# Gated cross-attention: the scalar engine's exponential moved ahead of the three copies of the unit before it

## What is computed

```
q = qn @ Wq * scale                          # 16 heads of 64
k, v = split(media @ Wkv)                    # 1500 keys
sim = einsum('bhid,bhjd->bhij', q, k)
sim = where(media_mask, sim, neg_inf)
attn = softmax(sim, axis=-1)
out = einsum('bhij,bhjd->bhid', attn, v)
x = x + tanh(attn_gate) * (out @ Wo)
x = x + tanh(ff_gate) * (gelu(layernorm(x) @ W1) @ W2)
```

## Time and profile before

| | |
|---|---|
| median of 3 runs | 2667.14 us (2666.37 to 2675.62) |
| the profiled execution's own time | 2673.55 us |
| its span, first to last instruction | 2671.8 us |
| PE busy | 2521.3 us (94% of the span) |
| DVE, ACT, POOL busy | 1572.3, 1258.2, 590.3 us |
| mean granted TensorE clock | 0.95 of full speed |
| the two stretches of gated attention | about 217 to 860 us and 1930 to 2570 us |

### The profile page before, as it was taken

The page is one execution under the profiler, slowest core; times in us unless marked ns, Lnnn a source line. Parts: engine busy times, 40 slices in busy tenths (PEclk is TensorE's granted clock), DMA queues, the critical chain, the costliest instruction groups (busy, mean ns, idle before and its releaser), DMA issues.

```text
span 2671.8 us, 43128 instructions
## 1 busy us (share of the span) xinstructions
PE 2521.3 (94%) x16890; PEld 2048.4 (77%) x16890; DVE 1572.3 (59%) x4305; ACT 1258.2 (47%) x2148; POOL 590.3 (22%) x729
## 2 busy tenths in 40 slices
PE   7779999999999988988999999899999999999998
PEld 4647999999999667965666666545599999999975
DVE  3146777777776233446766766521577777777741
ACT  2125555555555211116777777520455555555521
POOL 0013444444440004200000000000244444444200
PEclk8789999999999997569999999899999999999999
DMA  8511111111100200001000010101111111111010
GB/s 273 153 49 53 53 39 41 53 38 41 53 27 1 80 18 1 1 3 45 24 24 24 24 34 4 34 31 58 38 41 53 39 41 53 39 41 53 1 48 14
DMA packets 36103, 116.34 MB, mean 44 GB/s; under 512 B 4598, under 2 KB 18526, under 8 KB 35534
## 3 DMA queue, kind: packets, MB, share of 16 engines
q1 hardware_dynamic: 33438, 101.30, 12.2%
q10 hardware_dynamic: 2464, 12.29, 1.8%
HBM read 112.66 MB, written 0.92 MB: 43 GB/s over the span
## 4 chain that ended last, share of the span: by engine, by line
PE 86%; DVE 8%; ACT 2%; DMA 2%; issue 1%; POOL 0%; SPq 0%; ACTq 0%; DVEq 0%; POOLq 0%
PE bank L864 19%; PE bank L851 17%; PE bank L876 11%; DVE n_scores L1635 4%; PE bank L1516 4%; PE bank L1503 3%; PE bank L1528 3%; PE bank L1744 3%; PE bank L1088 2%; PE bank L1073 2%; PE bank L1272 2%; PE bank L683 2%; PE bank L1081 2%; PE bank L1754 2%; PE bank L1253 2%; PE bank L504 2%
## 5 line engine op out<-in xcount | busy, mean ns | idle before, releaser
L924 ACT CAST p_T_high<-bank 125x512 fp32r<-125x512 f32 x672 | 350.6, 595 | 546.8 <-PE bank L876 546.8
L1004 DVE TENSOR_TENSOR p_T_low<-bank,p_T_high 125x512 fp32r<-125x512 f32 x576 | 362.2, 684 | 183.0 <-ACT p_T_high L924 179.5
L864 PE MATMUL bank<-p_T_high,keys_nat_high 125*128 125x256 f32 x1536 | 419.3, 283 | 1.7 <-ACT inverse L931 1.7
L962 DVE CUSTOM_DVE_ANT_0 scores<-bank,mask 128x500 f32<-128x500 f32 x672 | 418.2, 672 | 1.5 <-PE bank L851 1.5
L864 PE MATMUL bank<-p_T_high,keys_nat_low 125*128 125x256 f32 x1536 | 419.1, 283 | 0.0
L934 ACT ACTIVATE scores<-scores,row_max 128x1500 f32<-128x1500 f32 x224 | 353.6, 1578 | 6.5 <-DVE row_max L967 6.5
L876 PE MATMUL bank<-ident,scores 128*125 128x128 f32 x2688 | 330.7, 272 | 1.3 <-ACT scores L934 1.3
L864 PE MATMUL bank<-p_T_low,keys_nat_high 125*128 125x256 f32 x1152 | 325.4, 282 | 0.0
L876 PEld LDWEIGHTS bank<-ident,scores 128*125 128x125 f32 x2688 | 314.2, 188 | 2.7 <-ACT scores L934 2.5
L1635 DVE CUSTOM_DVE_ANT_0 n_scores<-bank,n_zeros 112x500 f32<-112x500 f32 x384 | 237.5, 675 | 127.3 <-PE bank L1503 127.3
L864 PEld LDWEIGHTS bank<-p_T_high,keys_nat_high 125*128 125x128 f32 x1536 | 291.4, 190 | 10.1 <-ACT inverse L931 2.2
(11 more groups left out here) (209 smaller groups left out, 3649.2 us busy)
## 6 DMA issues: line engine op xcount, KB each, us to landing
ctx_T<-in_ctxT SPq DMA_DIRECT2D x40, 750.0 KB, 4.2
ctx_nat<-in_ctx SPq DMA_DIRECT2D x32, 672.0 KB
q_and_o<-in_ctxT SPq DMA_DIRECT2D x16, 750.0 KB, 10.4
q_and_o<-in_ctx ACTq DMA_DIRECT2D x16, 672.0 KB
mask_bytes<-in_mask SPq DMA_DIRECT2D x32, 187.5 KB, 3.0
n_ctx_T<-in_ctxT SPq DMA_DIRECT2D x8, 750.0 KB, 4.4
weights<-in_L_W SPq DMA_DIRECT2D x4, 1024.0 KB, 9.7
ctx_nat<-in_ctx SPq DMA_DIRECT2D x32, 78.0 KB
```

The source lines that it names most:

```text
L864: m = e.matmul(psum[6 + g % 2][:, 0:256], KNs[i][b % 2][0:KP, cols], PTs[j][g % 2][0:KP, k, :], start=(k == 0 and n == 0), stop=(k == KT - ...
L924: e.copy(PTs[0][g % 2][0:KP, 4 * c:4 * c + 4, lo:lo + 128], psum[3 + c][0:KP, :].rearrange("p (k r) -> p k r", k=4)).then_inc(s_eh, 1)
L962: e.tensor_tensor_reduce(out=SB[u % 2][:, c * CHK:(c + 1) * CHK], in0=psum[c][:, 0:CHK], in1=mb[:, c * CHK:(c + 1) * CHK], scale=1.0, scal ...
L1004: e.tensor_tensor(low, psum[3 + c][0:KP, :].rearrange("p (k r) -> p k r", k=4), high.bitcast(F32), ALU.subtract).then_inc(s_el, 1)
```

## The change

In every slot of `act_cross` the exponential of unit s is issued first, and after it the copies (and the inverse copy) of unit s-1. Nothing is added or taken away, and the programs of the other engines are as they were.

```diff
             for s in range(U + 1):
                 u = s - 1
+                if s < U:
+                    on.wait_ge(*x.negmax(s))
+                    e.activation(SB[s % 2], SB[s % 2], ACT.Exp, bias=mx[:, s % 4, 3:4],
+                                 accum_out=mx[:, s % 4, 4:5]).then_inc(s_ex, 1)
                 if u >= 0:
                     g = group_of(u)
                     lo = 128 * ((u % RT) % 2)
...
                         if g >= 2:
                             on.wait_ge(*x.o_out(g - 2))
                         e.copy(inverse[g % 2][:, 0:n], psum[6 + g % 2][:, 0:n]).then_inc(s_in, 1)
-                if s < U:
-                    on.wait_ge(*x.negmax(s))
-                    e.activation(SB[s % 2], SB[s % 2], ACT.Exp, bias=mx[:, s % 4, 3:4],
-                                 accum_out=mx[:, s % 4, 4:5]).then_inc(s_ex, 1)
```

## The result

The changed kernel takes 2749.96 us (median of 4 runs, 2746.35 to 2753.74), the kernel before 2666.76 us (4 runs): a ratio of 1.0312, 95% interval 1.0291 to 1.0333. That is 83 us more.

What follows compares the result with a forecast made beforehand. PE was taken to bound the kernel at 5.71 us a slot; a ring of 6.06 us adds 41.4 us a layer, 83 for two: 2673.55 + 83 = 2756.5 us profiled, 2750 as a median; range 2720 to 2800.

Steps and rivals of the forecast that it cites:

- What bounds the kernel: Layer 1's attention: PE busy 610.00 of 610.00 us, 5.71 us a slot, and waiting for no exponential.
- the ring: Gated attention: closed loop of maxima, negated maximum, exponential, copies, low parts, next maxima; 6.06 us a slot against PE's 5.71.
- from exponential to copy: Step on ACT between the starts of the exponential and of the copy behind it, taken as 1.54 us.
- Start to start or full lengths: Pricing of one turn: distances between starts give 6.06 us and 2750; full instruction lengths give 6.29 us and 2800.
- The inverse copy and DVE's results at no cost: ACT's inverse copy (0.41 us) and DVE's result of a group (0.42 us) were to add nothing to a slot.
- PE's waits: PE waits up to 1.1 us for the inverse, three times a batch: 2.4 us idle a batch, PE busy 94%.
- its rival: PE joins the ring: restarts costing 1.1 us would overrun by 0.9 us a batch, 29 us, 2779 us; chance 0.12.
- The clock: Rival: PE's idling lowers its clock for a tenth of the time, 98 us in all, 2848 us; chance 0.05.
- The sum: Gated stage of one layer: last unit's maxima move from 852.8 to 894.2 us, 41.4 us, 83 for two layers.

## Why the prediction was right

- **What bounds the kernel, and that an earlier exponential frees nobody:** right. PE was busy for all of 610 us, and the kernels in which the exponential is early but the ring short come to 1.0015 and 1.0030.
- **The ring and its length:** forecast 6.06 us, found 6.04, link by link 1.91, 0.19, 1.54, 0.60 and 1.80 against 1.91, 0.19, 1.54, 0.62 and 1.80. Only the step from copy to low part was 0.02 us too long. The one link with no row in the gated stage, from exponential to copy, had been taken from layer 2 and holds to the hundredth. That this ring is the cause is shown, not argued: opened in every second slot it costs nothing, a known length put in comes out whole (71 us for 72), and a shorter link ahead of the copies takes nearly all the loss away.
- **Start to start or full lengths:** the full lengths would have given 6.29 a slot and 2800 us; the 6.048 us between the negated maxima decides for the distances between starts. The rule of the Trainium skill that I had named ("Perfetto Trace Analysis", "Optimizing Scalar/DVE Operations") says the same, and the runs bear it out. The choice was worth 50 us.
- **The inverse copy and DVE's results at no cost:** right, with less to spare than forecast, which priced a group's result alone (0.42 us). For a single unit three instructions stand there, and the last of them lasted 1.22 or 1.24 us in place of 0.29 in 14 of the 15 batches from 240 to 880 us (609.81 in the timeline), each time beside a POOL instruction (here `keys_nat_low`, 609.59 to 610.88). It ended 0.32 us before the low parts started. The prediction had no term for this; that it stayed hidden is luck.
- **PE's waits:** 46 in 640 us, that is, in 15.1 batches of 42.3 us: three in a batch, right in place and number. The forecast was 2.4 us of idle in a batch and PE busy for 94%; PE's rows show 23.7 us of idle, 1.6 in a batch, and 96%. A batch is 42.3 - 40.0 = 2.3 us longer all the same. The 0.8 us that idle doesn't show are three restarts of 0.27 us, in which the profile has PE busy. The prediction gave them no price, named 1.1 us in its rival and saw the ring in danger above 0.6. At 0.27 the ring keeps its pace. That price was learnt from the kernel with one copy ahead; the runs with the longer ring show that the waits are no part of the cost.
- **The clock:** granted in full in both stages (PEclk 1.00), with PE busy for 96% of them. That rival did not come about.
- **The sum:** forecast 41.4 us for a layer, found 38.2 and 39.2. The turn is 0.012 us shorter than taken, 1.3 us over 109 turns. Of the other 1.9 us of layer 1, 1.7 lie in its first slots: the negated maxima of units 0 and 1 are at 219.97 and 221.95 now, 1.98 us apart, where they were 3.70 apart before, when the score matmuls of unit 1 started 0.42 us apart, at the lower clock, and not 0.23; the ring starts with unit 1. The prediction had taken that slower start over from the trace of before. In layer 3 that start was at full speed before as well (1923.15 and 1925.13, 1.98 apart). That the medians are 83 apart, just as forecast, while the stages grew by 77 in the profiled executions, is some luck.
- **Three steps of the experiments' expectations failed by size:** PE's restart after a wait (61 us where 31 were forecast), DVE's instruction meeting POOL's (144 us for 74), and the link behind half an exponential (0.92 us for 0.74). None touches the verdict on the change.

## What to carry to other kernels

Before swapping two instructions on an engine that has slack, follow each engine's own order through the semaphores and ask whether the swap closes a ring: here ACT was busy for 57% of the stage and DVE for 74% before the change, and yet the two together set the pace once each had to wait for the other in every slot. Add up the ring from start to start, and compare it with the slot of the engine that bounds; a fraction over costs that fraction in every slot, a fraction under costs nothing. Then look for further loops: the order with one copy ahead had a ring under PE's slot and still cost 61 us, through the inverse. In a stage that another engine bounds, an instruction that is early for its reader is worth nothing, while the one that it pushes back may be the next that somebody waits for.

## What the runs showed of the hardware that was not expected

- A DVE addition with both operands in SBUF (128 x 256) took 414 ns on average in one order and 727 ns in another. Where POOL was at work when it began, it ended 0.27 to 0.29 us after POOL's instruction (42 of 99) and lasted up to 1.61 us. With one operand in PSUM it lasted 0.41 or 0.42 us in all of 97, met by POOL or not, and the low parts (an operand in PSUM) 683 to 688 ns in the mean in every kernel. The Trainium skill ("SBUF — State Buffer", section "SBUF: two separate sides") has the rule: DVE and GpSimd share a pair of SBUF ports under an exclusive lock, and a DVE instruction with two SBUF inputs waits for the end of a GpSimd one that reads SBUF. The traces agree, with 0.27 to 0.29 us between the two ends. It also fits the 1.22 and 1.24 us of DVE's result for a single unit, whose operands both lie in SBUF: 128 x 128, with 0.14 to 0.16 us between the ends. It went the other way too: where the addition was under way first, POOL's `keys_nat_low` lasted 1.47 to 1.50 us in 13 cases (1.34 in one), and 1.27 to 1.29 elsewhere. A price for a DVE instruction in a ring is therefore good only for its phase against POOL.
- PE behind a wait of 0.32 us for ACT's inverse lost 0.27 us beyond it: 18 matmuls in 2.42 us in place of 2.15. Where the inverse came some 0.2 us before PE's scores ended (607.93 against 608.14), the sums still took 2.25 us: the profile shows the weight load, and not a matmul, waiting for the inverse.
- The exponential of 1500 columns lasted 1579 ns on average in the kernel before and 1548 in the changed one, and the copies 595 and 584, where the exponential no longer runs beside DVE's low parts and maxima. In the kernel with the ring closed in every second slot both stand side by side: 1548 for the 112 that go first, 1578 for the 112 that go last. Whether that is the reason is not shown.
